# Rests of v for two batches by negated-identity products and ScalarE, weights scaled in rounding, all orders rewritten

## The reference, cut to what matters

```
v = x @ W_write.T                      # the kernel folds W_read and alpha in: v = x @ comb
S = r @ w.T                            # r = x, w = x moved by one row
reads = (S * M) @ v                    # M: decay gamma**(distance) below the diagonal
x1 = layernorm(x + (x + alpha * reads @ W_read.T))
q(t) = grid(t / s) * s, s = max|t| / 6 per block of 16
h = silu(q(x1) @ q(w_gate).T) * (q(x1) @ q(w_up).T)
out = layernorm(x1 + q(h) @ q(w_down).T)
```

## Time and profile before

| | before |
|---|---|
| median of 3 runs | 326.03 us (325.96 to 326.42) |
| the profiled execution | 325.95 us |
| its span | 324.1 us |
| TensorE busy | 313.5 us, 97% |
| VectorE busy | 293.3 us, 91% |
| GpSimd busy | 242.0 us, 75% |
| ScalarE busy | 210.2 us, 65% |
| granted TensorE clock | 0.998 |

### The profile page before, as it was taken

The page is one execution under the profiler, slowest core; times in us unless marked ns, Lnnn a source line. Parts: engine busy times, 40 slices in busy tenths (PEclk is TensorE's granted clock), DMA queues, the critical chain, the costliest instruction groups (busy, mean ns, idle before and its releaser), DMA issues.

```text
span 324.1 us, 6506 instructions
## 1 busy us (share of the span) xinstructions
PE 313.5 (97%) x2061; PEld 284.2 (88%) x2061; DVE 293.3 (91%) x753; ACT 210.2 (65%) x515; POOL 242.0 (75%) x258
## 2 busy tenths in 40 slices
PE   8989999999999999999999999999999999999993
PEld 3979888979988999899999999999989889999983
DVE  4989898999898989698996989999999999999982
ACT  7458977594915786348926687467657745666774
POOL 1889859857975789956996688687677767569672
PEclk9999999999999999999999999999999999999999
DMA  6812300110010202020020200020001000001002
GB/s 227 297 69 67 120 11 0 68 66 2 1 65 18 82 2 79 20 81 20 32 68 16 83 1 33 2 81 15 20 2 33 16 2 33 19 16 34 33 18 80
DMA packets 8241, 15.68 MB, mean 48 GB/s; under 512 B 1040, under 2 KB 5136, under 8 KB 8208
## 3 DMA queue, kind: packets, MB, share of 16 engines
q1 hardware_dynamic: 7920, 15.01, 13.7%
q10 hardware_dynamic: 288, 0.26, 0.2%
HBM read 11.08 MB, written 4.19 MB: 47 GB/s over the span
## 4 chain that ended last, share of the span: by engine, by line
PE 73%; DVE 14%; issue 5%; ACT 4%; POOL 2%; ACTq 0%; DVEq 0%
PE gu L1703 11%; PE gu L1707 11%; PE gu L1704 11%; PE bank L1703 6%; PE bank L1707 5%; PE bank L1704 5%; PE bank L1791 4%; PE bank L1713 3%; PE bank L1717 3%; PE bank L1716 3%; DVE h_y L1075 2%; PE bank L1765 2%; DVE w_raw L1186 2%; PE gu L1716 2%; PE gu L1717 1%
## 5 line engine op out<-in xcount | busy, mean ns | idle before, releaser
L412 POOL TENSOR_TENSOR h_q<-h_g,h_ns 128x704 f32<-128x704 f32 x32 | 47.3, 1478 | 39.2 <-DVE h_g L1080 35.8
L1703 PE MATMUL gu<-guT_hi,xqT_hi 128*128 128x512 f32 (+1 forms) x192 | 74.8, 389 | 0.5 <-DVE w_raw L1186 0.5
L1704 PE MATMUL gu<-guT_lo,xqT_hi 128*128 128x512 f32 (+1 forms) x192 | 72.0, 375 | 0.0
L686 ACT ACTIVATE w_raw<-gu 128x512 f32<-128x512 f32 x64 | 29.3, 461 | 47.2 <-PE gu L1707 46.9
L1707 PE MATMUL gu<-guT_hi,xqT_lo 128*128 128x512 f32 (+1 forms) x192 | 56.7, 376 | 0.5 <-DVE xqT_lo L1177 0.5
L405 POOL TENSOR_TENSOR h_n<-w_raw,h_rs 128x704 f32<-128x704 f32 x32 | 49.0, 1532 | 9.5 <-DVE h_rs L1070 8.9
L1703 PEld LDWEIGHTS gu<-guT_hi,xqT_hi 128*128 128x128 f32 x192 | 36.1, 188 | 6.7 <-issue 1.3
L1707 PEld LDWEIGHTS gu<-guT_hi,xqT_lo 128*128 128x128 f32 x192 | 35.5, 188 | 6.7 <-DVE xqT_lo L1177 0.9
L1704 PEld LDWEIGHTS gu<-guT_lo,xqT_hi 128*128 128x128 f32 x192 | 36.1, 188 | 5.2
L1075 DVE SCALAR_TENSOR_TENSOR h_y<-h_sq,h_n 128x704 f32<-128x704 bf16 x34 | 36.3, 1069 | 1.7 <-ACT h_sq L690 1.7
L1186 DVE TENSOR_TENSOR w_raw<-w_raw,gu 128x512 f32<-128x512 f32 x64 | 32.2, 505 | 2.9 <-ACT w_raw L686 2.1
(11 more groups left out here) (158 smaller groups left out, 940.4 us busy)
## 6 DMA issues: line engine op xcount, KB each, us to landing
xs<-in_x_rows_dram SPq DMA_DIRECT2D x8, 512.0 KB, 3.3
out_dram<-wq_gu SPq DMA_DIRECT2D x32, 128.0 KB, 1.7
x_full<-in_xt_rows_dram SPq DMA_DIRECT2D x7, 512.0 KB, 3.2
w_raw<-in_w_ffn_dram SPq DMA_DIRECT2D x6, 352.0 KB, 6.6
w_pair<-in_w_attn_dram SPq DMA_DIRECT2D x1, 512.0 KB, 5.1
...
scal<-in_scalars_dram ACTq DMA_DIRECT2D x1, 1.0 KB, 1.7
```

Source lines behind the costliest of these rows:

```text
L412: nc.gpsimd.tensor_tensor(blocks(h_q[:, p, 0:I]), blocks(h_g[:, p, :]), per_block(h_ns[:, p, :], HB), ALU.mult).then_inc(h_quant, 1)
L686: nc.scalar.activation(silu[:, p, part[half]], gate_of[half], ACT.Silu).then_inc(silu_ready, 1)
L1703: nc.tensor.matmul(dst, lh, rh, start=(first and i == 0), stop=False)
L1704: nc.tensor.matmul(dst, lh, rl, start=False, stop=False)
```

## The change

Five things change.

1. For batches 0 and 1, `v_rest` is dropped. A new `v_subtract(n, u)` on TensorE adds `v_hi` times the negated identity to v's bank (one product of 512 columns), and a new `v_remainder` on ScalarE copies the bank to `v_lo`. Batches 2 to 7 keep `v_rest`. `values` now opens one accumulation group in its bank instead of one for each half.
2. `x_rest` of batch 1 moves from GpSimd to VectorE.
3. `scale_comb` is dropped. `round_comb` scales while it rounds, `rest_comb` scales and subtracts in one instruction. `combine` writes bank 1 instead of bank 3.
4. The tables of banks change.
5. The lists of all five engines are written in another order, and the `body` of the loop begins at another point of the cycle.

```diff
-        comb = sb("comb", [P, DK * D])
-        v_bank, xq_bank = (bank[2], bank[1]), (bank[1], bank[3])
-        s_bank, r_bank = (gu[:, 3, :], bank[0], bank[3], gu[:, 3, :]), (bank[2], bank[1])
-        h_bank = ((bank[1], bank[0]), (bank[1], bank[0]), (bank[2], gu[:, 3, :]), (bank[3], gu[:, 3, :]))
-        d_bank = (bank[3], bank[0], bank[2], gu[:, 3, :])
+        v_bank, xq_bank = (bank[2], bank[0]), (bank[1], bank[3])
+        s_bank, r_bank = (gu[:, 3, :], bank[0], bank[3], gu[:, 3, :]), (bank[1], bank[0])
+        h_bank = ((bank[1], bank[0]), (bank[1], bank[2]), (gu[:, 3, :], bank[2]), (bank[3], bank[2]))
+        d_bank = (bank[3], bank[0], gu[:, 3, :], gu[:, 3, :])
...
             def round_comb():
-                act.wait_ge(comb_ready, 1)
-                nc.scalar.copy(comb_hi[:].rearrange("p c d -> p (c d)"), comb[:]).then_inc(comb_hi_ready, 1)
+                act.wait_ge(comb_filled, 1)
+                act.wait_ge(act_consts, 2)
+                nc.scalar.activation(comb_hi[:].rearrange("p c d -> p (c d)"), bank[1][:, 0:DK * D], ACT.Copy,
+                                     scale=scal[:, 3:4]).then_inc(comb_hi_ready, 1)
...
+            def v_remainder(n, u):
+                act.wait_ge(v_left, 2 * n + u + 1)
+                c = slice(2 * u, 2 * u + 2)
+                nc.scalar.copy(v_lo[:, c, :].rearrange("p i d -> p (i d)"), v_bank[u][:]).then_inc(v_lo_ready, 1)
...
             def v_rest(n, u):
                 dve.wait_ge(v_hi_ready, 2 * n + u + 1)
+                if n == 2 and u == 0:
+                    dve.wait_ge(v_lo_ready, 4)
...
             def rest_comb():
                 dve.wait_ge(comb_hi_ready, 1)
-                nc.vector.tensor_tensor(comb_lo[:].rearrange("p c d -> p (c d)"), comb[:],
-                                        comb_hi[:].rearrange("p c d -> p (c d)").bitcast(F32),
-                                        ALU.subtract).then_inc(comb_lo_ready, 1)
+                nc.vector.scalar_tensor_tensor(comb_lo[:].rearrange("p c d -> p (c d)"), bank[1][:, 0:DK * D], scal[:, 3:4],
+                                               comb_hi[:].rearrange("p c d -> p (c d)").bitcast(F32), ALU.mult,
+                                               ALU.subtract).then_inc(comb_lo_ready, 1)
...
+            def v_subtract(n, u):
+                c = slice(2 * u, 2 * u + 2)
+                pe.wait_ge(v_hi_ready, 2 * n + u + 1)
+                nc.tensor.matmul(v_bank[u][:], neg_ident[:], v_hi[:, c, :].rearrange("p i d -> p (i d)"), start=False,
+                                 stop=True, skip_group_check=True).then_inc(v_left, 1)
...
             scores(0, 1, [])
-            scores(0, 2, [(comb_ready, 1)])
-            scores(0, 3, [(pr_ready, 1)])
+            scores(0, 2, [])
             pe.wait_ge(comb_lo_ready, 1)
             values(0, 0, [])
-            values(0, 1, [])
-            reads(0, 0, [(v_lo_ready, 1)])
+            scores(0, 3, [(pr_ready, 1)])
+            v_subtract(0, 0)
+            values(0, 1, [(pr_ready, 2)])
+            reads(0, 0, [(comb_lo_ready, 1)])
+            v_subtract(0, 1)
             scores(1, 0, [(pr_ready, 4)])
...
             down(28, 0, [(hT_lo_ready, 55)])
-            h_transpose(30, 2, 0, [(o_ready, 27)])
-            h_transpose(30, 2, 1, [(o_ready, 28)])
-            down(29, 1, [(hT_lo_ready, 60)])
+            h_transpose(30, 2, 0, [(o_ready, 28)])
+            down(29, 1, [(hT_lo_ready, 58)])
+            h_transpose(30, 2, 1, [(hT_lo_ready, 60)])
+            down(30, 2, [(hT_lo_ready, 61)])
             h_transpose(31, 3, 0, [(o_ready, 29)])
             h_transpose(31, 3, 1, [(hT_lo_ready, 62)])
-            down(30, 2, [(hT_lo_ready, 61)])
-            down(31, 3, [(hT_lo_ready, 64)])
+            down(31, 3, [(o_ready, 31)])
```

More of the change, by code:

```diff
@@ new lines, in _ @@
+            hidden(3, 1, 0)
+            h_magic_add(1, 1)
+            x_magic_add(1, 1)
+            decay_scores(3, 1)
+            decay_scores(3, 2)
+            hidden(3, 1, 1)
+            h_to_grid(1, 1)
+            x_maxima(2, 0)
+            h_maxima(3, 1)
+            h_rest(0, 0, 0)
+            h_rest(0, 0, 1)
+            hidden(4, 0, 0)
+            h_divisors(3, 1)
+            h_magic_add(2, 0)
+            x_to_grid(1, 1)
+            h_to_grid(2, 0)
+            x_moments(2, 1)
@@ new lines, in _ @@
+            hidden(4, 0, 1)
+            h_reciprocals(3, 1)
+            h_rest(1, 1, 0)
+            out_residual(0, 0)
+            v_rest(3, 0)
+            h_maxima(4, 0)
+            hidden(5, 1, 0)
+            h_magic_add(3, 1)
+            h_divisors(4, 0)
+            decay_scores(3, 3)
+            h_reciprocals(4, 0)
+            xq_rest(1, 1)
+            out_moments(0, 0)
+            x_divisors(2, 0)
+            x_reciprocals(2, 0)
+            h_to_grid(3, 1)
+            h_rest(1, 1, 1)
@@ new lines, in _ @@
+            hidden(5, 1, 1)
+            x_residual(3, 0)
+            v_rest(3, 1)
+            h_maxima(5, 1)
+            hidden(6, 0, 0)
+            h_magic_add(4, 0)
+            x_maxima(2, 1)
+            x_divisors(2, 1)
+            h_divisors(5, 1)
+            out_residual(1, 1)
+            x_reciprocals(2, 1)
+            h_rest(2, 2, 0)
+            x_magic_add(2, 0)
+            h_reciprocals(5, 1)
+            x_to_grid(2, 0)
+            decay_scores(4, 0)
+            decay_scores(4, 1)
@@ L1539, in _ @@
-            out_moments(15, 1)
+            decay_scores(7, 3)
+            h_to_grid(18, 0)
+            hidden(20, 0, 0)
+            hidden(20, 0, 1)
+            h_maxima(20, 0)
+            h_rest(17, 1, 0)
+            out_moments(15, 1)
+            out_residual(16, 0)
+            h_divisors(20, 0)
+            h_magic_add(19, 1)
+            x_magic_add(6, 0)
+            h_to_grid(19, 1)
+            x_to_grid(6, 0)
+            x_divisors(6, 1)
+            h_reciprocals(20, 0)
+            hidden(21, 1, 0)
@@ new lines, in _ @@
+            h_maxima(24, 0)
+            hidden(25, 1, 0)
+            xq_rest(6, 1)
+            h_divisors(24, 0)
+            h_to_grid(23, 1)
+            hidden(25, 1, 1)
+            out_residual(19, 3)
+            h_reciprocals(24, 0)
+            x_reciprocals(7, 0)
+            h_rest(20, 0, 1)
+            h_rest(21, 1, 0)
+            h_maxima(25, 1)
+            h_divisors(25, 1)
+            h_reciprocals(25, 1)
+            out_moments(19, 1)
+            h_rest(21, 1, 1)
+            x_maxima(7, 1)
@@ new lines, in _ @@
+            reads(3, 0, [(hT_lo_ready, 3)])
+            h_transpose(1, 1, 1, [(v_lo_ready, 7)])
+            h_transpose(2, 2, 0, [(pr_ready, 16)])
+            gate_up(6, 1, 2, 0)
+            gate_up(6, 1, 2, 1)
+            down(1, 1, [(v_lo_ready, 8)])
+            gate_up(7, 1, 3, 0)
+            h_transpose(2, 2, 1, [(hT_lo_ready, 4)])
+            h_transpose(3, 3, 0, [(xqT_lo_ready, 4)])
+            scores(4, 0, [(hT_lo_ready, 5)])
+            scores(4, 1, [(o_ready, 2)])
+            down(2, 2, [(pr_ready, 17)])
```

1342 lines of the change are left out of this document (625 added, 717 removed).

## The result

The changed kernel takes 327.88 us, median of 5 runs (327.66 to 328.46), beside 326.02 us (325.96 to 326.42, 5 runs) of the kernel before on the same chip. The ratio is 1.0048, 95% interval 1.003 to 1.0066: slower by half a per cent. The forecast was 327.5 us, its range 324.5 to 329.8. The profiled execution took 328.08 us with a span of 326.3 us, 2.2 us more than before.

What follows compares the result with a forecast made beforehand. TensorE was taken as the bound, busy 313.5 of 324.1 us, with VectorE second. Terms 0.92 + 0.4 - 1.0 + 1.2 = +1.5 us gave 327.5 us; own range 326.7 to 328.5, whole range 324.5 to 329.8 us.

Steps and rivals of the forecast that it cites:

- behind the last product: After TensorE's last product: the residual had waited for ScalarE, and up to 0.2 us of that may go.
- part 1 of the prediction: Batches 0 and 1: four v_subtract products cost TensorE 0.92 us; VectorE loses 2.7 us, ScalarE gains 2.3 us.
- Hidden by nothing: The four new products' 0.92 us counts in full, since TensorE has no slack.
- Alpha (part 2): Weights scaled in rounding: scale_comb's 0.707 us on VectorE goes, and TensorE's wait of about 0.2 us goes.
- part 3: Start up to 37 us: x rests held by GpSimd, partly given back; +0.4 us, bounds -0.6 and +1.6.
- give-back: Start: a TensorE late from the held x rests finds later inputs ready, such as v_lo(1, 0), sparing about 0.65 us.
- part 4: Middle, 37 to 303 us: some shown waits go, one new 0.3 us wait; -1.0 us, bounds -2.5 and +2.0.
- part 5: End: TensorE stands between transposes of tiles 30 and 31 and their products; +1.2 us, from +0.6 to +2.2.
- Relief carries through: Rival: lighter VectorE ends every middle wait on it, -2.1 us, x rests not held; 324.8 us, chance 0.24.
- New close pairs: Rival: new short distances repeat in the loop, +2.0 us in the middle; 329.6 us, chance 0.16.
- Nothing shows: Rival: the middle gives back 2.5 us, the rest as forecast; 326.0 us, chance 0.18.

Runs made afterwards that it cites:

- e1: Changed kernel with v_rest of batches 0 and 1 back on VectorE, v_subtract and v_remainder gone: 329.88 us, ratio 1.0107.
- e11: Changed kernel with VectorE again scaling the weights' product by alpha in a separate instruction ahead of the first decay: 328.18 us, ratio 1.0057.
- e2: Changed kernel with VectorE's two x rests of batch 1 ahead of the rounding of weight unit 1: 328.04 us, ratio 1.0045.
- e8: Changed kernel with the two x rests of batch 1 back on GpSimd, ahead of w_dequant(1): 327.90 us, ratio 1.0049.
- e9: Changed kernel with ScalarE's tile 30 rounding ahead of two output normalisations and three places of VectorE reordered: 326.84 us, ratio 1.0019.
- e3: Changed kernel with ScalarE's rounding of tile 30's last transposes ahead of two output normalisations: 327.08 us, ratio 1.002.
- e4: Kernel before with down(30) ahead of the transposes of tile 31: 329.00 us, ratio 1.0073.
- e5: Changed kernel with down(30) behind tile 31's transposes again, VectorE's out_residual(30) behind tile 31's rests: 330.65 us, ratio 1.0131.
- e6: Changed kernel with the second half of gate_up(31) ahead of down(26), other engines following, down(30) behind tile 31's transposes, its output in bank 0: 328.82 us, ratio 1.0077.
- part 2 alone: Kernel before with only the x rests of batch 1 moved from GpSimd to VectorE, ahead of w_magic_add(1): 325.67 us, ratio 0.9987.

## Why the prediction was right, and where its terms were not

The side and the mechanism at the largest place were right. The terms, in profiled executions:

| term | forecast | measured |
|---|---|---|
| four products | +0.92 | +0.92 |
| waits up to 37 us | +0.4 | -0.24 |
| 37 to 303 us | -1.0 | -0.22 |
| from 303 us | +1.2 | +2.03 |
| behind the last product | 0 | -0.31 |

The products' row is 4 x 0.23 us on both sides; what two of them take more stands in the row below it. Without the late clock of the first products that row would be about -0.5. The forecast's nearness, 327.5 against 327.88 us, is in part luck: the start came 0.6 us below its term, the middle and the end 0.8 us each above theirs.

**The products (part 1 of the prediction).** The distance to the next start is 0.23 us at two of them, 0.34 us at the two that follow a wait. "Hidden by nothing" held. e1 adds what the sum could not show: in this order they pay for themselves.

**Alpha (part 2).** The wait of 0.2 us was forecast to go and the values to begin at 11.3 us; they began at 11.49. e11 confirms that the path is short: VectorE's 0.65 us appear as 0.46. Its worth at the end is 0.3 us at most.

**The start (part 3).** The held x rests are as drawn: at 16.78 us (16.75 forecast), over at 19.25 us (19.4), TensorE released at 19.30 (19.4). The rule of the Trainium skill ("SBUF — State Buffer", section "SBUF: two separate sides"), an exclusive lock for a whole instruction, agrees again with this row, and with e2, where the same pair takes 1.41 us. What failed is the price: I took half a microsecond and more of it as lasting. e2 and e8 show it worth nothing, since waits for `decay_scores` took its place in both (1.03 us at 18.75 us in e2, 0.32 us at 22.48 us in e8). The give-back was the larger part.

**The middle (part 4).** The step that failed: that shown waits go and leave their time. Of the 2.0 us in the four rows that name VectorE nothing is left, and the one new wait that part 4 listed came as forecast, 0.34 us at 48.06 us behind a silu and its product. But 1.6 us of other waits for VectorE came too, at 76.8, 217.0 and 225.5 us, which part 4 did not see. e9 is the nearest sight of the reason: take a wait from TensorE, and VectorE, which has no pause there, is met again 5 us on. That VectorE's pace sets the sum in the whole middle is argued from this and e11, not shown. e11 says it from the other side, 0.46 us late at 11 us is 0.01 us late at 217 us.

**The end (part 5).** The step was mis-sized: 1.07 us before `down(31)` measured 1.00; 0.65 us before `down(30)` measured 1.44, of which 0.7 us are ScalarE's two normalisations (e3), which the prediction had in its upper bound and did not take. This is most of the 0.8 us missing. Its cause was read too narrowly as well. The prediction blamed the place of `down(30)`; e4 shows that this place alone does cost 1.7 to 2.0 us in the old banks, but e5 that in the new order undoing it costs more. There tile 31's last `h_q` comes 3.3 us later than before, because VectorE's reciprocals for it stand at 310.47 us, not 305.74. They follow the second half of `gate_up(31)`, now behind `down(26)`. e3 ends with this chain and TensorE level. Whether an order exists that brings the chain forward without holding up tiles 29 and 30 stays open: e6 did not find one. So of the 2.0 us at the end 0.6 to 0.8 are shown by an experiment; the 1.0 us ahead of `down(31)` is seen in the trace, and no run takes it away.

**Rivals.** "Relief carries through" failed in the middle: 3.1 us less of VectorE's busy time gave 0.2 us there. "New close pairs" came true in part, one wait for another, but without a growth of the sum. (Its own sum is loose: eight waits of 0.35 us are 2.8 us, not 2.0, and it does not say why the ends then cost 1.0 us less.) "Nothing shows" needed 2.5 us from the middle.

Of all that was tried, the kernel before with part 2 alone is the fastest, 325.67 us. In the order in which it came, part 2 shows no worth.
